# Layer-0 row bias from a GpSimd product and a VectorE row sum, in place of six matmuls

## The reference

```python
# layer 0: the softmax runs over the 512 queries, not over the context
q = x @ Wq + bq;  k = ctx @ Wk + bk;  v = ctx @ Wv + bv
w = softmax((q @ k.T) / 16, axis=queries)
x1 = layernorm(w @ v + x) * gamma + beta
# layer 1: the softmax runs over the context
Q = x1 @ Wq1 + bq1;  K = ctx @ Wk1 + bk1;  V = ctx @ Wv1 + bv1
out = x1 + softmax((Q @ K.T) / 16, axis=context) @ V @ Wo + bo
```

## Time and profile before

| | us |
|---|---|
| median of 3 runs | 517.94 |
| lowest, highest | 516.08, 518.86 |
| span of the profiled execution, first to last instruction | 511.7 |
| median of the runs less that span | 6.24 |

### The profile page before, as it was taken

How to read it: one execution, slowest core, us unless ns; L and a number is a source line. 1 busy time by engine, 2 the same in 40 slices (tenths; PEclk the granted TensorE clock), 3 DMA queues, 4 the chain that set the end, 5 groups by cost and what they waited for, 6 DMA issues and landing times.

```text
span 511.7 us, 7981 instructions
## 1 busy us (share of the span) xinstructions
PE 464.3 (91%) x2426; PEld 381.0 (74%) x2426; DVE 387.2 (76%) x920; ACT 385.2 (75%) x798; POOL 346.2 (68%) x319
## 2 busy tenths in 40 slices
PE   8659887999989998999899998999899998799776
PEld 8447555888778886888688885888688886587675
DVE  2355579769986899769977898679976998669744
ACT  3576956998689967997789966987799867872452
POOL 0195966896787948896688857896689768971400
PEclk9989978999999999999999999999999999999989
DMA  8400030000040005000140005000220001000101
GB/s 241 114 0 1 1 106 0 2 2 0 7 141 2 1 1 146 3 0 1 33 115 1 1 2 147 1 0 1 66 83 0 2 3 41 0 1 10 34 0 42
DMA packets 23897, 17.31 MB, mean 34 GB/s; under 512 B 1055, under 2 KB 23854, under 8 KB 23854
## 3 DMA queue, kind: packets, MB, share of 16 engines
q1 hardware_dynamic: 23850, 16.79, 11.4%
q10 hardware_dynamic: 4, 0.00, 0.0%
HBM read 12.59 MB, written 4.19 MB: 33 GB/s over the span
## 4 chain that ended last, share of the span: by engine, by line
PE 41%; DVE 36%; ACT 8%; issue 8%; DMA 4%; POOL 2%; SPq 0%; DVEq 0%; POOLq 0%; ACTq 0%
DVE p1T_lo L884 7%; PE ps_s L432 5%; DVE xr L938 5%; PE ps_l L432 5%; PE ps_l L433 5%; PE ps_s L434 5%; PE ps_l L434 5%; PE ps_s L433 5%; DMA x_sb<-in_x_dram 4%; DVE xr L899 4%; PE ps_s L546 4%; DVE s_sb L872 3%; DVE max L951 3%; DVE y_res L978 2%; DVE xhat L930 2%
## 5 line engine op out<-in xcount | busy, mean ns | idle before, releaser
L1069 POOL TENSOR_TENSOR p_lo<-p,p_hi 128x512 fp32r<-128x512 f32 (+1 forms) x104 | 135.2, 1307 | 83.4 <-ACT p_hi L750 83.4
L1062 POOL TENSOR_TENSOR wsum<-wsum,p 128x512 f32<-128x512 f32 (+1 forms) x88 | 115.0, 1307 | 4.6 <-ACT p L742 1.3
L736 ACT ACTIVATE p<-s_sb,min 128x512 f32<-128x512 f32 (+1 forms) x104 | 75.3, 725 | 18.8 <-DVE min L872 16.8
L884 DVE TENSOR_TENSOR p1T_lo<-ps_s,p1T_hi 128x512 fp32r<-128x512 f32 (+1 forms) x104 | 68.0, 681 | 26.7 <-ACT p1T_hi L787 26.5
L787 ACT CAST p1T_hi<-ps_s 128x512 fp32r<-128x512 f32 (+1 forms) x104 | 59.1, 585 | 30.7 <-PE ps_s L546 18.1
L872 DVE CUSTOM_DVE_ANT_0 s_sb<-ps_l,cb 128x512 f32<-128x512 f32 (+1 forms) x104 | 69.8, 683 | 12.5 <-PE ps_l L434 8.9
L742 ACT ACTIVATE p<-p,r 128x512 f32<-128x512 f32 (+1 forms) x104 | 73.1, 719 | 4.4 <-DVE r L879 3.9
L951 DVE TENSOR_REDUCE max<-ps_s 128x1 f32<-128x804 f32 x60 | 59.1, 994 | 15.7 <-PE ps_s L434 13.3
L750 ACT CAST p_hi<-p 128x512 fp32r<-128x512 f32 (+1 forms) x104 | 63.4, 618 | 1.3 <-PE ps_l L434 0.7
L546 PE MATMUL ps_s<-ident,p 128*128 128x128 f32 (+1 forms) x416 | 58.7, 279 | 5.0 <-ACT p L779 5.0
L546 PEld LDWEIGHTS ps_s<-ident,p 128*128 128x128 f32 (+1 forms) x416 | 50.4, 145 | 14.6 <-ACT p L779 7.3
(11 more groups left out here) (163 smaller groups left out, 1063.8 us busy)
## 6 DMA issues: line engine op xcount, KB each, us to landing
ctx_sb<-in_ctx_dram SPq DMA_DIRECT2D x24, 256.0 KB, 4.9
x_sb<-in_x_dram SPq DMA_DIRECT2D x8, 512.0 KB, 4.2
out_dram<-y_res SPq DMA_DIRECT2D x16, 256.0 KB, 2.2
p<-in_L_xattn_Wq_dram SPq DMA_DIRECT2D x2, 256.0 KB, 3.7
ctx_sb<-in_ctx_dram SPq DMA_DIRECT2D x8, 32.5 KB
p<-in_L_xattn_Wk_dram SPq DMA_DIRECT2D x2, 128.0 KB, 3.8
p<-in_L_xattn_Wv_dram SPq DMA_DIRECT2D x2, 128.0 KB, 4.3
p<-in_L_xattn_Wo_dram SPq DMA_DIRECT2D x1, 256.0 KB, 4.7
```

The source lines that it names most:

```text
L736: nc.scalar.activation(p0[0:m, ring0(i), :], s0_sb[0:m, (a.par + i) % 2, :], ACT.Exp, bias=min0[0:m, i:i + 1], scale=-1.0, accum_out=sum0[ ...
L884: nc.vector.tensor_tensor(p1T_lo[0:m, i % RING, :], ps_turn[i % 3][0:m, :], p1T_hi[0:m, i % RING, :].bitcast(F32), ALU.subtract).then_inc( ...
L1062: nc.gpsimd.tensor_tensor(total, total, p0[0:m, ring0(i), :], ALU.add).then_inc(wsum_done, 1)
L1069: nc.gpsimd.tensor_tensor(p0_lo[0:m, h, :], p0[0:m, ring0(i), :], p0_hi[0:m, h, :].bitcast(F32), ALU.subtract).then_inc(p0_lo_done, 1)
```

## The change

The row bias is no longer formed on TensorE from the turned x. GpSimd multiplies x (all four blocks of 128 queries, 1024 elements in a partition) with u as a row (`weigh_u0`, into `xr`), VectorE adds each block's 256 products (`sum_z0`, into `z0`, 128 x 4), and TensorE transposes each column of `z0`, repeated 128 times, so that the sums stand in a row on all partitions. `bias0` and `max0` are as before. `sum_z0` stands directly behind `q0_low` and ahead of `rowmax1` 4; `weigh_u0` stands behind `sum_weights` 7 and ahead of `p0_low` 6.

```diff
 VECTOR_ORDER
-    ("recip0", "a", 8), ("recip0", "a", 9), ("q0_low", "c", 0), ("rowmax1", "b", 4), ("rowmax1", "b", 5),
+    ("recip0", "a", 8), ("recip0", "a", 9), ("q0_low", "c", 0), ("sum_z0", "c", 0), ("rowmax1", "b", 4), ("rowmax1", "b", 5),
 GPSIMD_ORDER
-    ("sum_weights", "a", 5), ("ctx_low", "a", 3), ("sum_weights", "a", 6), ("sum_weights", "a", 7), ("p0_low", "a", 6),
+    ("sum_weights", "a", 5), ("ctx_low", "a", 3), ("sum_weights", "a", 6), ("sum_weights", "a", 7), ("weigh_u0", "c", 0), ("p0_low", "a", 6),
...
             def project_bias0(a, _):
-                for c in range(EC):
-                    mm = split3(ps_misc[:], u0_hi[:, c, :], u0_lo[:, c, :], xT_hi[:, c, :], xT_lo[:, c, :],
-                                start=(c == 0), stop=(c == EC - 1))
+                pe.wait_ge(z0_done, a.n + 1)
+                for t in range(TB):
+                    mm = nc.tensor.transpose(ps_misc[:, t * P:(t + 1) * P], z0[:, t:t + 1].broadcast_to([P, P]), ident[:])
                 mm.then_inc(cb_ps, 1)
...
 (TensorE, once, before the first body: two matmuls of 256 columns in place of four of 128)
-                for c in range(EC):
-                    for h in range(EC):
-                        mm = nc.tensor.matmul(s1_bank(2)[:, E + c * P:E + (c + 1) * P], wqT[0][:, h, c * P:(c + 1) * P],
-                                              bk_rep[0][:, h, :], start=(h == 0), stop=(h == EC - 1))
+                for h in range(EC):
+                    mm = nc.tensor.matmul(s1_bank(2)[:, E:2 * E], bk_rep[0][:, h, :], wqT[0][:, h, :],
+                                          start=(h == 0), stop=(h == EC - 1))
...
 (ScalarE, x_turned: the wait before xT_hi is written again)
-                    act.wait_ge(cb_ps, a.n)
+                    act.wait_ge(qw0_ps, a.n)
 (ScalarE, once)
-                nc.scalar.copy(u0_hi[:].rearrange("p c l -> p (c l)"), s1_bank(2)[:, E:2 * E]).then_inc(made_sb, 1)
+                nc.scalar.copy(u0_row[:], s1_bank(2)[:, E:2 * E]).then_inc(u0_done, 1)
...
+            def sum_z0(a, _):
+                dve.wait_ge(xu0_done, a.n + 1)
+                if not first(a):
+                    dve.wait_ge(cb_ps, a.n)
+                nc.vector.tensor_reduce(z0[:], xr[:], AX_X, ALU.add).then_inc(z0_done, 1)
...
 (VectorE, bias_x0, before it writes xr)
+                if not last(a):
+                    dve.wait_ge(z0_done, a.n + 2)
 (VectorE, once)
-                weight_low(u0_lo[:].rearrange("p c l -> p (c l)"), s1_bank(2)[:, E:2 * E],
-                           u0_hi[:].rearrange("p c l -> p (c l)"))
...
+            def weigh_u0(a, _):
+                pool.wait_ge(x_loaded[a.par], 16 * (a.use + 1))
+                if first(a):
+                    pool.wait_ge(u0_done, 1)
+                elif a.n == 1:
+                    pool.wait_ge(z0_done, a.n)
+                else:
+                    pool.wait_ge(c1_done, TB * (a.n - 1))
+                nc.gpsimd.tensor_tensor(xr[:], x_sb[a.par][:], u0_row[:].unsqueeze(1).broadcast_to([P, TB, E]), ALU.mult
+                                        ).then_inc(xu0_done, 1)
```

More of the change, by code:

```diff
@@ L206, in xattn_kernel @@
         a1_gamma = sb("a1_gamma", [P, EC, P])
-        u0_hi, u0_lo = (sb(f"u0_{part}", [P, EC, P], F32R) for part in ("hi", "lo"))
+        u0_row = sb("u0_row", [P, E])
+        z0 = sb("z0", [P, TB])
         wv0_hi, wv0_lo = (sb(f"wv0_{part}", [P, E], F32R) for part in ("hi", "lo"))
@@ L328, in xattn_kernel @@
         var_done = sem("var_done")
+        u0_done, xu0_done, z0_done = sem("u0_done"), sem("xu0_done"), sem("z0_done")
         ctx_lo_done, wsum_done, y_part_done, y_res_done = (
@@ L511, in turn_y @@
                     pe.wait_ge(row1_made, MADE)
-                    pe.wait_ge(weights_lo_done, 3)
+                    pe.wait_ge(weights_lo_done, 2)
                 for t in range(TB):
@@ L623, in pre0 @@
                 pe.wait_ge(small_sb, 1)
-                pe.wait_ge(weights_lo_done, 2)
+                pe.wait_ge(weights_lo_done, 1)
                 pe.wait_ge(xT_lo_done, EC)
@@ L652, in pre1 @@
                     nc.tensor.matmul(s1_bank(0)[:, 0:1], wkT[:, 1, h, :], bq_col[1][:, h:h + 1], start=(h == 0), stop=False)
-                pe.wait_ge(made_sb, 3)
+                pe.wait_ge(made_sb, 2)
                 for c in range(EC):
@@ L1000, in pre0 @@
                 xT_low(batch(0, 0), 1, s1_bank(3))
-                dve.wait_ge(made_sb, 2)
+                dve.wait_ge(made_sb, 1)
+                dve.wait_ge(u0_done, 1)
                 weight_low(a0_lo[:].rearrange("p c l -> p (c l)"), s1_bank(2)[:, 0:E], a0_hi[:].rearrange("p c l -> p (c l)"))
-                weight_low(u0_lo[:].rearrange("p c l -> p (c l)"), s1_bank(2)[:, E:2 * E],
-                           u0_hi[:].rearrange("p c l -> p (c l)"))
                 ctxT_low(batch(0, 0), 0)
@@ L1013, in pre1 @@
                 nc.vector.tensor_tensor(betaob_part, beta_row, bo_row, ALU.add).then_inc(row1_made, 1)
-                dve.wait_ge(made_sb, 4)
+                dve.wait_ge(made_sb, 3)
                 for c in range(EC):
@@ L1021, in pre1 @@
                 weight_low(wv0_lo[:], wv0_sb, wv0_hi[:])
-                dve.wait_ge(made_sb, 5)
+                dve.wait_ge(made_sb, 4)
                 dve.wait_ge(row1_made, 1)
@@ L1032, in _ @@
             steps = {f.__name__: f for f in (
-                ctxT_low, xT_low, at0_low, bias_x0, q0_low, max0, recip0, residual0, moments0, normalised, bias_row1, q1_low, rowmax1, bias1_of, recip1, p1_low, finish)}
+                ctxT_low, xT_low, at0_low, bias_x0, q0_low, sum_z0, max0, recip0, residual0, moments0, normalised, bias_row1, q1_low, rowmax1, bias1_of, recip1, p1_low, finish)}
             def body(a, b, c, done=()):
@@ L1101, in _ @@
             steps = {f.__name__: f for f in (
-                ctx_low, sum_weights, p0_low, rsqrt_var, residual1)}
+                ctx_low, sum_weights, p0_low, rsqrt_var, weigh_u0, residual1)}
             def body(a, b, c, done=()):
```

## The result

The changed kernel takes 523.18 us (median of 4 runs, 521.13 to 526.67), the kernel before on the same chip 517.32 (4 runs). The ratio is 1.0112, 95% interval 1.0067 to 1.0158: slower, by 5.9 us. (Every ratio in this text is taken from the recorded runs by one rule; the quotient of the two medians can differ from it by up to 0.0024.) The prediction said 523.2 us, range 519.3 to 528.5, and gave "slower" 0.79.

What follows compares the result with a forecast made beforehand. The prediction took a chain across engines, with TensorE waiting for `exp1` 4 at the edit, to bound full bodies. First body 0.15, c = 1 1.8 and full bodies 3.3 give 5.25 us on 517.94: 523.2 us, range 519.3 to 528.5.

Steps and rivals of the forecast that it cites:

- Part 2: VectorE's sum in six full bodies: 1.13 us of queue delays `rowmax1` 5 by 0.55 us each, 3.3 us in all.
- Part 3: GpSimd's product in full bodies: 2.4 us, hidden by the gap ahead of `p0_low` 7 and the exponential, price 0.
- Parts 1 and 4: TensorE: some 1.0 us freed per body wins 0 in full bodies; transposes end before `scores1` 12 can start, price 0.
- Part 6: First body: sum and transposes delay `cb` by 0.15 us; bounds 0 and 1.0, the upper if TensorE returns at half clock.
- The rival in which TensorE is the bound: The wait of `scores1` 12 is only TensorE's queue, so freed time counts: 8.0 us won, 509.9 us; chance 0.06.
- Part 5: Body with c = 1, where GpSimd sets the end: the product adds 1.8 us, bounds 0 and 2.4.
- 6.24 us around the span: Whole kernel: the median of the runs lies 6.24 us above the profiled span of 511.7 us.
- The rule weighed: VectorE's sum: a `tensor_reduce` never contends with GpSimd for the shared port pair, so it stays at 1.13 us.
- the blocked sum: The sum waits for the GpSimd instruction in flight, 0.75 us more in each full body: 527.7 us; chance 0.08.
- Hidden: The sum fits before the maximum and the first bodies absorb the product: 518 us, no gain; chance 0.12.
- GpSimd falls behind: A product of 3.0 us or more delays tiles after `p0_low` 7, some 0.4 us per full body: 525.6 us; chance 0.06.
- The clock falls: TensorE's longer idle time between 215.4 and 217.6 lowers its clock, 1 us a body: 529.2 us; chance 0.04.

Runs made afterwards that it cites:

- The sum alone: Kernel before plus a VectorE row sum over x behind `q0_low`, result unused, six matmuls kept, no product: 527.17 us, ratio 1.0153.
- the sum ahead of `q0_low`: Changed kernel with the sum moved ahead of `q0_low` and the product ahead of `sum_weights` 5: 515.66 us, ratio 0.9974 to the kernel before.
- the matmuls taken away alone: Kernel before with the six matmuls replaced by four transposes of zeros, no product or sum, row bias left out: 513.38 us, ratio 0.993.
- The shorter product alone: Kernel before plus a GpSimd product of x with itself at the place of `weigh_u0`, result unused, six matmuls kept: 518.05 us, ratio 1.0016.
- the kernel before with the moved scores: Kernel before, six matmuls kept, with only `scores0` 11 moved behind `weigh0` 7: 519.43 us, ratio 1.002.
- the sum twice: Changed kernel with a second, equal sum directly behind the first: 539.26 us, ratio 1.0411 to the kernel before.
- the four forms: Changed kernel, sum ahead of `q0_low`: plain 0.9974; `scores0` 11 moved 0.9924; item 1's product in the first body, with that move 0.9938, without 0.9953.

## Why the prediction was right

**Part 2, VectorE's sum.** Right in mechanism and size. Predicted queue time 1.13 us, measured 1.13; predicted delay 0.52 by the sum, taken as 0.55, measured 0.53. The sum alone reproduces it, and the sum ahead of `q0_low` removes it. (The bound of 0.82 without any overlap comes to 0.78 by the same rows; nothing hangs on it.) One thing was missed: I took all six full bodies to be like the one at 198. In the body c = 2, GpSimd reaches the product only 1.5 us ahead of `q0_low`, and the product is the later one, by 0.2 us. The chain of the kernel after there:

```profile
100.17 2.42 POOL xr L1103
...
102.61 1.22 DVE z L869
```

It is 0.78 us in that body and not 0.55. The other 0.5 of its +1.3 lies ahead of `turn_x`. There TensorE's clock is low in all four traces, and lower after: over the first 8 us from the load it is 0.76 and 0.76 before, 0.61 and 0.57 after. That the 0.5 us are this clock's is likely and not shown.

**Part 3, the product in full bodies.** Right: 2.40 us by its line, predicted 2.4; the gap is gone; alone it gives a ratio of 1.0016 and no longer segment in bodies c = 3 to 7. Its price of 0 fails in c = 2, as just told.

**Parts 1 and 4, TensorE.** Right for full bodies. The transposes end before `exp1` 4 releases `scores1` 12, and with the matmuls taken away alone no full body becomes shorter. The kernel without them was 4.8 us faster by its medians; 1.0 of that is the first body, where I had counted TensorE's relief within Part 6, and most of the rest goes with a higher clock, as told there. The rival in which TensorE is the bound would have put 1.0 us into every body and is refuted for c = 3 to 7; outside them TensorE's work does cost time, 1.0 us in the first body.

**Part 5, the body with c = 1.** Right: predicted 1.8, measured 1.7. The product runs from 51.11, and GpSimd then works without a gap to the last sum of weights, which starts at 66.07 and not at 63.37; 1.0 of these 2.7 us the body was late already at its `q0_low`. The shorter product alone gives 1.2, and no product in that body gives 0.5 less than before.

**Part 6, the first body.** `q0_low` to `cb` grew from 2.50 to 2.68, +0.18, predicted 0.15. What stands before it costs nothing, as predicted: from the first `turn_x` to `q0_low` it is 8.72 to 8.73 us in all four traces, though by the landing of x all of it is some 0.4 earlier in those of after. What was missed lies behind `cb`: from there to `q0_low` of c = 1 it is 32.4 and 32.5 us before and 33.9 in both traces of after, +1.4. This is TensorE's clock. The windows of before, then of after:

```profile
32.00:36.00 4.00, 0.78 (x3) 0.78 (x4) 3.96 (x7) 3.17 (x8) 3.86 (x4) 0.87 0.00 0
36.00:40.00 4.00, 4.00 (x18) 3.55 (x17) 1.09 (x4) 0.65 (x2) 2.90 (x3) 0.71 0.00 0
```

```profile
32.00:36.00 4.00, 0.46 (x2) 0.47 (x3) 3.70 (x6) 3.48 (x10) 3.86 (x4) 0.65 0.00 0
36.00:40.00 4.00, 4.00 (x15) 3.46 (x15) 1.97 (x2) 0.65 (x2) 3.10 (x3) 0.50 0.00 0
```

The rows of the second traces show where it starts, before and after. TensorE waits 5.25 us for ScalarE in either kernel, and what follows runs at half clock for a while:

```profile
35.12 2.07 PE L588 MATMUL ps_s<-p 128*128 128x128 f32 x8 [5.25 <-ACT p L817]
```

```profile
35.05 2.08 PE L590 MATMUL ps_s<-p 128*128 128x128 f32 x8 [5.26 <-ACT p L818]
```

From this row to `turn_x` of c = 1 it is 8.43 and 8.50 us before, at a mean granted clock of 0.82. It is 9.19 at 0.76 and 9.91 at 0.70 after, 10.04 at 0.69 with the sum alone, 9.91 at 0.70 with the product alone, 8.64 at 0.81 without the matmuls, 8.97 at 0.78 in the kernel before with the moved scores. Length times clock is 6.9 to 7.0 us in all thirteen traces: the work is the same, and the clock sets its time.

In the first trace of after the clock fell once more, from 19.5 to 23.0, which is the other 0.7 of its +1.4 (16.98 us from `cb` to the end of the 5.25 us of waiting, 16.28 to 16.29 in both of before and in the second of after). That is the upper bound of this part come true: the sum lengthens TensorE's wait ahead of the transposes from 1.71 to 2.92 us, and in one of the two traces a fall came behind it. With the sum twice the wait is 4.18 us, and the clock is at 0.50 from 18 to 24. Why the clock stays down longer after the 5.25 us in some forms than in others stays open; it isn't one added instruction, since the kernel before with the moved scores alone has 0.5 us of it.

**Sum.** 5.25 predicted. The medians differ by 5.9, interval 3.5 to 8.2. The traces differ by 8.0, since both of before are from its short end. The larger missing terms are the 1.4 behind the first body and 0.7 in c = 2, to which the prediction gave no time. Against that, the median execution of before is longer than its traces by more (some 4 us) than that of after (some 1.5). So the mechanism and its size were right, but it is luck that 523.2 meets 523.18: the median of before moved from 517.94 to 517.32 with one more run, and the 2.7 us that the sum lacks in the traces (8.0 against 5.25) shrank to 0.6 by which executions the medians hold. What I called 6.24 us around the span was in truth 2.1 us of surroundings (513.79 us of time over 511.7 of span, in the second trace) and some 4 us by which the profiled execution was shorter than the median; a forecast by difference doesn't feel this.

**The rule weighed.** The Trainium skill (SBUF — State Buffer, section Who interferes with whom) says that a `tensor_reduce` on this chip never contends with GpSimd. The eight sums of 1207 to 1221 ns agree, and seven of them ran wholly beside GpSimd's work. In the body at 202.8 the sum, 217.12 to 218.33, ran beside `p0_low` 6 and 7, 216.69 to 219.25, and began without a wait, which rules the blocked sum out.

**The other rivals.** Hidden: refuted, the segment grew. GpSimd falls behind: refuted for `p0_low`, and true by 0.2 us in one body, at the product itself. The clock falls: TensorE idles 0.98 to 1.11 us where I had looked, and its clock stays at 1.00 behind that in all full bodies of both traces. But the margin is small: with the sum twice it fell there in four of six. It falls elsewhere, after the 1.33 us at the head of a body, and does so in the kernel before too. Why the sum alone has this fall in all of bodies c = 3 to 7, and the whole change in none or one, no run settled. Its bodies are 57.93 to 57.98 us long for it, those of the first trace after 57.09 to 57.59, which is a part of the difference between +9.0 and +5.9 us.

## What to carry to other kernels

Work taken off the busiest engine is worth what stands in the chain at that place: six matmuls that filled a wait gave nothing in the repeating bodies (and 1.0 us in the first, where TensorE itself was waited for), while a 1.1 us instruction put ahead of the last releaser cost half its length in each. Before adding work to an engine, look for its idle time in the same stretch: the same sum one place earlier in the order costs nothing in bodies c = 3 to 7, though some 0.5 us where c = 1. With it the change turned from 1.1% slower to 0.3% to 0.8% faster (the four forms' ratios; the first can't be told from no change, and two of the others also move `scores0` 11). Check each kind of body, the first ones too, and compare differences of traces with differences of medians, since one execution can be 1% from the median. When they disagree, compare executions with a like mean granted clock first.

## What was unexpected of the hardware

- The same idle time of TensorE (1.33 us) is followed by full clock in one body and by 1.2 GHz for 3 us in the next (matmuls of 402 columns at 0.34 and 0.54 us). From the load to `turn_x` it is then 4.92 us and not 3.81, and part of the lost time hides behind the landing of x.
- A wait of TensorE can be followed by a fall of the clock in one body and not in the next: 0.98 to 1.11 us behind the transposes left it at 1.00 in all twelve full bodies of the two traces after, while 1.11 us with 1.4 to 1.5 us ahead of the transposes brought 0.50 in four of six.
- After one and the same wait of 5.25 us the clock came back at different times: the same work took 8.43 to 10.04 us, and that length times the mean granted clock was always 6.9 to 7.0 us.
- A GpSimd product of x with itself took 1.90 us, that of x with a row read four times 2.40, both over 1024 elements; which difference of the inputs it is wasn't separated.
